# Half words, a new order and four more one-hots on ScalarE in round B; row tables laid out before layer 0 and cleared beside it

## The reference

```python
h = relu(layernorm(x))
x = x + L0(h, W, Bv, src, dst, edge_type)     # 8 x 8 matrix by edge type, summed over dst (6250 nodes of 128)
h = relu(layernorm(x))
# layer 1; edge_index = [src, dst]
w = relu(edge_attr @ w1 + b1) @ w2 + b2       # 320 weights of each edge
msg_s = einsum('ei,eij->ej', x[dst], wa);  msg_v = einsum('ei,eij,ec->ejc', x[dst], wb, sh1)
out = segment_mean(concat(msg_s, msg_v), src); s0, v0 = batch_norm(out)
w = relu(edge_attr @ w1' + b1') @ w2' + b2'
path_a = einsum('ei,eij->ej', s0[dst], wa);  path_b = einsum('eic,ec,eij->ej', v0[dst], sh1, wb)
x = x + batch_norm(segment_mean(path_a + path_b, src))
```

## Time and profile before

| | us |
|---|---|
| median of three runs | 23958.75 |
| span of the profiled execution | 23994.0 |
| stretch 2060 to 10700 (round A) | 8640 |
| stretch 13530 to 23900 (round B) | 10370 |
| VectorE busy in the span | 19509.6 (81%) |
| GpSimd busy | 15973.0 (67%) |
| TensorE busy | 15946.4 (66%) |
| ScalarE busy | 10304.8 (43%) |

### The profile page before, as it was taken

The page is one execution under the profiler, slowest core; times in us unless marked ns, Lnnn a source line. Parts: engine busy times, 40 slices in busy tenths (PEclk is TensorE's granted clock), DMA queues, the critical chain, the costliest instruction groups (busy, mean ns, idle before and its releaser), DMA issues.

```text
span 23994.0 us, 483073 instructions
## 1 busy us (share of the span) xinstructions
PE 15946.4 (66%) x137837; PEld 9487.0 (40%) x137837; DVE 19509.6 (81%) x37328; ACT 10304.8 (43%) x23410; POOL 15973.0 (67%) x18227
## 2 busy tenths in 40 slices
PE   5232777777777777766666577766777777777675
PEld 2221333333333333335656333333343333433333
DVE  8114888888888888889999888888888888888888
ACT  1001444444444444449999433333333333333332
POOL 0772777777777777777777566666666666666665
PEclk6555888888888888877777788888888888888887
DMA  4223333333333333324444222121222222222221
GB/s 142 52 50 132 111 111 106 110 111 111 106 109 111 111 107 109 111 97 118 118 118 118 65 40 40 40 40 40 40 40 40 40 40 40 40 40 40 40 40 37
DMA packets 1355296, 1864.35 MB, mean 78 GB/s; under 512 B 497379, under 2 KB 1137507, under 8 KB 1298789
## 3 DMA queue, kind: packets, MB, share of 16 engines
q1 hardware_dynamic: 835620, 1342.87, 18.2%
q0 software_dynamic: 483776, 469.85, 9.2%
q10 hardware_dynamic: 35842, 50.96, 0.6%
HBM read 1452.58 MB, written 409.77 MB: 78 GB/s over the span
## 4 chain that ended last, share of the span: by engine, by line
DVE 42%; issue 23%; POOL 16%; DVEq 6%; DMA 4%; ACT 3%; PE 3%; ACTq 1%; POOLq 1%; SPq 0%
POOL rows_d L731 13%; DVE arena L1767 11%; DVE arena L1716 7%; DVE arena L1774 6%; DVE arena L1758 5%; DMA rows_d<-arena 4%; DVEq L1794 4%; POOL arena L622 3%; DVE arena L1723 3%; ACT arena L1204 2%; DVE arena L1789 2%; DVE arena L1649 1%; DVE arena L1748 1%; DVE arena L1751 1%; PE wide L978 1%
## 5 line engine op out<-in xcount | busy, mean ns | idle before, releaser
L622 POOL DMA_INDIRECT arena<-s_tab,arena x7072 | 6703.2, 948 | 3772.1 <-issue 2032.1
L731 POOL DMA_INDIRECT rows_d<-arena x6656 | 6424.9, 965 | 2426.7 <-issue 2309.7
L1053 PE MATMUL wide<-w,arena 64*128 64x320 f32 x14144 | 3202.5, 546 | 2843.6 <-DVE arena L1758 2840.6
L978 PE MATMUL wide<-w,arena 64*128 64x320 f32 x13312 | 2975.3, 536 | 2257.1 <-DVE arena L1640 1639.7
L1649 DVE TENSOR_REDUCE arena<-arena 128x40 f32<-128x640 f32 x3328 | 2693.5, 809 | 428.3 <-DMA rows_d<-arena 427.6
L1640 DVE TENSOR_TENSOR arena<-wide,arena 128x640 f32<-128x640 f32 x3328 | 2653.0, 818 | 235.8 <-PE wide L978 167.0
L1053 PEld LDWEIGHTS wide<-w,arena 64*128 64x128 f32 x14144 | 1265.6, 210 | 3954.1 <-issue 2198.5
L1758 DVE TENSOR_TENSOR arena<-wide,arena 128x640 f32<-128x640 f32 x3536 | 2807.3, 815 | 0.2 <-PE wide L1053 0.2
L1767 DVE TENSOR_REDUCE arena<-arena 128x32 f32<-128x640 f32 x3536 | 2780.7, 806 | 0.0
L978 PEld LDWEIGHTS wide<-w,arena 64*128 64x128 f32 x13312 | 1189.1, 209 | 3150.7 <-issue 1778.3
L1039 PEld LDWEIGHTS duo<-ident_sb,arena 128*64 128x64 f32 x14144 | 1623.4, 175 | 1107.9 <-issue 1107.9
(11 more groups left out here) (208 smaller groups left out, 26899.6 us busy)
## 6 DMA issues: line engine op xcount, KB each, us to landing
arena<-rows_d SPq DMA_DIRECT2D x3536, 172.0 KB, 2.3
arena<-in_attr SPq DMA_DIRECT2D x208, 1024.0 KB
arena<-rel SPq DMA_DIRECT2D x208, 1024.0 KB
arena<-in_attr_rows SPq DMA_DIRECT2D x208, 768.0 KB
arena<-s_tab,arena POOLq DMA_INDIRECT x7072
rows_d<-arena POOLq DMA_INDIRECT x6656
rows_d<-zero ACTq DMA_DIRECT2D x198, 172.0 KB, 1.8
side<-arena SPq DMA_DIRECT2D x16, 1040.0 KB
```

Source lines behind the costliest of these rows:

```text
L622: pool.indirect_dma_start(out=dst_, out_offset=None, in_=tab, in_offset=bass.IndirectOffsetOnAxis(ap=idx, axis=0)).then_inc(signal, 16)
L731: pool.indirect_dma_start(out=rows_d[t // 4], out_offset=bass.IndirectOffsetOnAxis(ap=ui[:, s % GPT, t:t + 1], axis=0), in_=M[:, s % GPT, ...
L978: last = pe.matmul(wide[k % 2][:, j, 0:WN], hT[half, s % 2, k * P:(k + 1) * P], w2_sb[0][half, :], start=True, stop=True)
L1053: last = pe.matmul(wide[k % 2][:, j, 0:WN], bhT[half, s % 2, k * P:(k + 1) * P], w2_sb[1][half, :], start=True, stop=True)
```

## The change

**Round B.** The messages, their first and second rest lie beside each other as float32 (`bmsg[..., q, :]`), and TensorE takes the upper 16 bits of each word as its bf16 part (`bupper`, every second half word). The two casts on ScalarE go. VectorE builds four one-hots (`BACK_DVE`), ScalarE four. On VectorE the small instructions stand between the large ones: the vectors of g+1 (`turn_vectors`, `vectors`) are computed in group g, both bin numbers are loaded together ahead of `join`, and the two additions follow later. The semaphores that free `brow` and `bxg` change with that. TensorE's order in round B stays.

**Row tables.** VectorE lays out the tables before layer 0, and TensorE's two matrix products for it stand there too. ScalarE writes and reads the bin list before layer 0, and clears one bin (two transfers) after each of layer 0's first 96 groups, the rest after the loop.

```diff
@@ VectorE, round B
-                def prepare(g, s, it):
+                def turn_vectors(g, s, it):
                     dve.wait_ge(R.gathered[s], 16 * TPG * it + 16 * TPG)
...
-                    dve.wait_ge(R.vec, 2 * g + 1)
+                       ... ALU.mult).then_inc(R.vec_terms, 1)
+                def vectors(g, s):
+                    dve.wait_ge(R.vec_terms, g + 1)
                     red(bxg[:, s, :, 28:32], vtmp, AX, ALU.add).then_inc(R.vec, 1)
-                def rest0(g, s):
-                    dve.wait_ge(R.cast0, g + 1)
-                    tt(brest[:, s % 2], bmsg[:, s % 2], bparts[:, s % 2, :, 0], ALU.subtract).then_inc(R.rest, 1)
+                def rest0(g, s, first):
+                    dve.wait_ge(R.red, 4 * g + 4)
+                    if not first:
+                        dve.wait_ge(R.summed, g - 1)
+                    tt(bmsg[:, s % 2, :, 1, :], bmsg[:, s % 2, :, 0, :], bupper[:, s % 2, :, 0, :], ALU.subtract).then_inc(R.rest, 1)
...
                 def body(...):
...
-                        prepare(g, s, it)
-                        if not f:
-                            rest0(g - 1, before)
                         multiply(g, s, 0, f)
+                        if not f:
+                            rest0(g - 1, before, first and s < 3)
                         multiply(g, s, 1, f)
                         reduce_(g, s, 0, first and s < 2)
                         if not f:
                             rest1(g - 1, before)
                         multiply(g, s, 2, f)
                         reduce_(g, s, 1, False)
-                        hot_nodes(g, s, first and s < 2)
+                        if joins:
+                            at = bins_of(g - 2)
+                            join(g - 2, two, first and s < 3)
+                        hot_nodes(g, s, it, first and s < 2)
                         multiply(g, s, 3, f)
                         reduce_(g, s, 2, False)
+                        if joins:
+                            add(g - 2, 0, at[0])
+                        if more:
+                            turn_vectors(g + 1, (s + 1) % GPT, it + (s + 1) // GPT)
                         reduce_(g, s, 3, False)
-                        dve.wait_ge(R.red, 4 * g + 4)
-                        dve.wait_ge(R.hot, g + 1)
-                        dve.sem_inc(R.x_free, 1)
-                        dve.sem_inc(R.rows_free, 1)
-                        if not (first and s < 2):
-                            add(g - 2, (s - 2) % GPT)
+                        if joins:
+                            add(g - 2, 1, at[1])
+                        if more:
+                            vectors(g + 1, (s + 1) % GPT)
@@ ScalarE, round B
-                            cast0(g - 1, (s - 1) % GPT, first and s < 3)
                             relu(g + 1, (s + 1) % GPT, first and s == 0)
-                            cast1(g - 1, (s - 1) % GPT)
+                        squares(g, s, it)
                             copy_attr(g + 2, (s + 2) % GPT)
-                        squares(g, s, it)
                         hot_nodes(g, s, first and s < 2)
@@ SyncE and GpSimd, round B
-                            sp.wait_ge(R.rows_free, g - (GPT - 1))
-                            sp.wait_ge(R.hot_too, g - (GPT - 1))
+                            sp.wait_ge(R.vec_terms, g - (GPT - 1))
+                            sp.wait_ge(R.hot, g - (GPT - 1))
+                            sp.wait_ge(R.hot_dve, g - (GPT - 1))
-                            pool.wait_ge(R.x_free, g - (GPT - 1))
+                            pool.wait_ge(R.prod, 4 * g - 4 * (GPT - 1))
@@ ScalarE, layer 0
+            act.wait_ge(laid_out, 1)
+            act.dma_start(bin_d.rearrange("(h p j) -> p h j", h=2, j=8), gbin).then_inc(bin_out, 16)
...
             def out_copies(it, wide, clears):
...
                     last.then_inc(R.out_ready, 1)
+                    if clears:
+                        clear_bin(g)
```

249 lines of the change are left out of this document (126 added, 123 removed).

## The result

The changed kernel takes **22245.9 us** (median of 4 runs, 22243.0 to 22247.3), the one before 23958.7 us on the same chip (4 runs, 23956.6 to 23959.5): a ratio of 0.9286, 95% interval 0.9273 to 0.9299, 1713 us less.

A forecast was written before the change was run, and what follows sets the result against it. Round B was taken as bound by VectorE's program of 11.72 us a group, to become 10.75 through the TensorE loop. Round B 857, passage 226, layer 0 0: 1083 us less, 22876 us; range 22280 to 23270.

The forecast's parts named there:

- Clears off the passage: Passage to round A: without ScalarE's clears ahead of it, VectorE starts at about 2029 instead of 2254.51, 226 us less.
- Layer 0 took the clears for nothing: Layer 0, ScalarE's queue: two clears a group, 2.75 us, costed at nothing; 264 us if not hidden, chance 0.05.
- Laying out: Row tables laid out ahead of layer 0 instead of before round A: 0, at most 5 us.
- ScalarE cost nothing: Round B, ScalarE: from 4.2 to 6.0 us a group, covered by 4 us free, so no cost.
- the half words: Round B, `nodes` matmuls reading every second place: even twice as long, they would take 1 us of TensorE's slack.
- GpSimd's floor: Round B, GpSimd: eight gathers and the step between groups take 10.1 us a group, the next floor, 1430 us saved.
- VectorE's own program: Round B, VectorE's instructions alone: 8.9 us a group, 9.55 with the loads' stall and the loop's branch.
- they can run beside one reduction (0.73): Round B, before the join: two register loads of 1.1 to 1.2 us overlap one reduction, delaying the join about 0.5 us.
- the sign: Round B, VectorE: the join was to start 1.2 to 1.3 us after the start of the second reduction.
- my formula: Round B's loop through TensorE: way back averaging 6.9 us, third to last multiplication 3.65, branch and jitter 0.2: 10.75 a group.
- the stand before `weights` 1 grows by the 0.5 us of the loads: Round B, TensorE's idle time before `weights` 1: grows by 0.5 us instead of shrinking, an argument against the GpSimd-bound rival.
- the rival: Round B bound by GpSimd's 10.1 us a group as the clock rises: 22303 us, up to 22560; chance 0.30.

The follow-up runs named there:

- e_tables: Kernel before with only the row tables' half (laid out before layer 0, cleared beside it), round B as before: 23737.2 us, ratio 0.9906.
- e_fill_six_b: Changed kernel with six of eight gathers a group in round B and five unread matmuls in TensorE's stand before `weights` 1: 21141.1 us.
- e_loads: Changed kernel with one wait more: the two register loads start only once the multiplication ahead of them has finished: 23134.6 us.
- e_ahead_b: Kernel before with only the two register loads moved ahead of the same group's one-hots, rerun on an undisturbed chip: 22990.7 us, ratio 0.9596.
- e_loads_six_b: Changed kernel with register loads waiting for the multiplication ahead and six of eight gathers a group, rerun on an undisturbed chip: 23152.1 us.
- e_six: Changed kernel with six of eight gathers a group in round B, the other work all done: 21985.9 us.
- e_fill_loads_six: Changed kernel with six of eight gathers, register loads waiting for the multiplication ahead, and five unread matmuls in TensorE's stand: 21947.1 us.
- e_hot6_b: Changed kernel with six one-hots a group on VectorE and two on ScalarE in round B, rerun on an undisturbed chip: 22983.8 us.
- e_fill: Changed kernel with all eight gathers and five unread matmuls in TensorE's stand before `weights` 1: 22262.9 us, ratio 0.9288.

## Why the prediction was wrong, step by step

**Right.** Clears off the passage: 226 forecast, 230.0 in the trace, 223 by e_tables, with the wait of 10 to 12 us that was named (10.97). Of the 230.0, 3.5 are layer 0's earlier end, which e_tables does not have. Layer 0 took the clears for nothing. Laying out took some 20 us ahead of layer 0; GpSimd had its first gathers to do meanwhile and then waited 1.02 us for the first copy (it ran at 648.9, the sum had 646.5), but the first scatter still starts no later than before (650.0 for 651.2). ScalarE cost nothing: TensorE never stood idle before the hidden layer or the turning. Nor did the half words: a matmul of `nodes` took 184 ns on average, before 190. (These matmuls are bf16 by this kernel's choice and not by a need of TensorE: the others of the round are f32.) GpSimd's floor was put at 10.1 and is 10.02. VectorE's own program was put at 8.9 us without the stall of the loads and the loop's branch, and is 8.78 with what is left of both at full clock (e_fill_six_b).

**The step that failed: "they can run beside one reduction (0.73). So the join starts about 0.5 us late".** The price of the loads was nearly right: 1.1 to 1.2 us with their steps, 1.30 in the chain of e_loads. Their cover was wrong. I had them begin when the reduction begins, and took a join 1.2 to 1.3 us after that as the sign; it came after 0.80. The queue here goes on before what stands ahead of it has run, and so starts the loads with the third multiplication: 1.47 us of cover over 1.30 us of loads. In the kernel before, the first load of a group stood behind the wait for the join, with nothing running beside it, and the second behind the first addition alone. That second one could have warned me. This is the addition ahead of the load of the earlier trace rows:

```profile
18012.47 0.23 DVE L1798 TENSOR_TENSOR T<-T,arena 128x64 f32 x1 [0.85 <-DVE arena L1789]
```

The load begins at 18012.60, 0.13 us into an addition of 0.23: it did not wait for the end of what stood ahead of it. I chose the cover without using that row and without a second value beside it. e_ahead_b shows the removal (1.11 us a group), e_loads the return (1.02 us a group over GpSimd's floor, 1.34 over the loop).

**The second, with it: the clock was held fixed.** With a stall of 0.83 us my formula gives 10.75 + 0.33 = 11.08 us a group; e_loads_six_b has 11.02, and its two parts fit as well (3.98 and 7.1 by the formula, 4.01 and 7.02 in the trace). With a stall of 0.07 it gives 10.75 - 0.43 = 10.32, and e_six has 9.70. The missing 0.6 us lie on the way back (7.1 by the formula, 6.54 in the trace), and what e_fill_six_b and e_fill_loads_six show of that way is the clock: at 0.99 to 1.00 it is 5.64 and 5.69 us, whatever the stall. I took 0.83 and the mean parts of the kernel before on both sides, but stand and clock move together: stands before `weights` 1 of 2.82, 2.70 and 1.98 us went with 0.81, 0.82 and 0.85 (e_loads_six_b, e_hot6_b, e_six). The prediction expected 0.80 to 0.84 in the changed round; it was 0.86. It also used "the stand before `weights` 1 grows by the 0.5 us of the loads" as the reason against the rival. That reason was the failed step over again, so it could not serve as a second witness; the stand, 2.11 us in the median group of the kernel before, is 2.06 in the changed one.

**The rival was right**, with 0.30: GpSimd bound, VectorE waiting for gathers, GpSimd's idle time in pieces of 0.30 us. Its reason, a clock that rises, was only half of it: the clock rose to 0.86, and with the loads' stall it would have stayed at 0.81 and the loop at 11.02 us (e_loads_six_b), well above GpSimd's floor, as would be the 10.32 of the formula with the stall gone and the clock as it was. Its time, 22303, was 57 us high: 0.08 us a group (10.1 for 10.02) are 71 us. The range's low end, 22280, was taken from this rival with only 23 us of room below it. A floor worked out from "eight gathers plus a step between groups" needed both ends (with the step and without), and 9.98 without it would have put the end at 22200.

## What to carry to other kernels

Register loads began here while what stood ahead of them was still running, unless a wait stood ahead: put them where no wait stands ahead and two large operations run beside them, and look for them first where an engine's idle time is put down to itself. In a loop of two engines a microsecond saved on the one side was worth 1.6 (0.71 us of one-hots were 1.13 us of loop, 0.85 us of stall 1.33), since a shorter stand of TensorE went with a higher clock; a sum that holds the clock fixed came out right at the one stall (11.08 for 11.02) and 0.6 us too long at the other. And where two bounds are 0.3 us apart, as 9.70 and 10.02 here, the range has to reach below the lower side of the nearer one.

## What the runs showed of the hardware

- Two register loads with their steps (1.30 us in the queue) run beside the arithmetic that stands ahead of them: 0.07 us visible in the changed kernel, against 0.83 us when a wait lets them begin at a multiplication's end only (e_loads).
- Behind a stand of 2.09 us TensorE was at the lower level (hidden layer 2.08 us instead of 1.12); 1.38 us of matmuls that nobody reads, put into the stand, went with a granted clock of 1.00 in the round and gave 845 us (e_fill_six_b against e_six); with all eight gathers the clock was 0.99 and the time stayed (e_fill).
- The same 6656 scatters of round A took 8420 to 8452 us from the first to the last, the shortest of them 954 or 957 ns, from one execution to another and whatever the kernel.
- On one chip TensorE paused 0.5 to 2.6 us inside series of matmuls and the kernel before took 28603 us; the order of two kernels was reversed there. Its cause stays open.
